# Mixing lora_B by the gate: one plain F32 product against two F32R products of high and low parts

## The reference

```
y = conv1d(x, weight 9 taps, 4 groups) + cond @ c_weight.T + bias
base = y @ kernel (2048x2048) + ffn_bias
A_eff = einsum('bn,nri->bri', gate, lora_A)     # gate 8x16, one-hot
B_eff = einsum('bn,nor->bor', gate, lora_B)     # lora_B 16 x 2048 x 32
delta = B_eff (A_eff y) + lora_B_shared (lora_A_shared y)
out = x + base + delta
```

## Time and profile before

| | us |
|---|---|
| median of 3 runs | 1721.45 (1720.89 to 1723.88) |
| the profiled execution | 1724.4 |
| its span, first to last instruction | 1722.6 |
| TensorE busy | 1705.0 |
| VectorE busy | 1056.6 |
| ScalarE busy | 670.0 |
| TensorE waits of phase 0's convolutions for L997 / L903 | 2.2 / 0.6 |

### The profile page before, as it was taken

One profiled execution on the slowest core, in us unless ns is written; L12 is line 12 of the kernel. 1 busy time (PEld: TensorE's weight loads), 2 busy tenths in 40 slices (PEclk: granted clock), 3 DMA queues, 4 the chain that ended last, 5 costly groups with the idle time before them and its releaser, 6 DMA issues.

```text
span 1722.6 us, 21836 instructions
## 1 busy us (share of the span) xinstructions
PE 1705.0 (99%) x8498; PEld 1442.8 (84%) x8498; DVE 1056.6 (61%) x1428; ACT 670.0 (39%) x846; POOL 37.0 (2%) x70
## 2 busy tenths in 40 slices
PE   8899999999999999999999999999999999999998
PEld 6688888887888898999998888888888888888887
DVE  7677877674444679888886444454555545464443
ACT  6756666644222466566552112132323211121110
POOL 0001111010000000000000000000000000000000
PEclk9899999999999999999999999999999999999999
DMA  7869766675656658776666565577766898887764
GB/s 208 254 213 336 279 229 243 220 268 175 240 211 200 225 200 298 284 258 240 232 236 256 206 248 196 190 221 249 235 223 212 299 335 301 308 316 248 254 235 158
DMA packets 180142, 419.45 MB, mean 244 GB/s; under 512 B 50692, under 2 KB 90212, under 8 KB 175400
## 3 DMA queue, kind: packets, MB, share of 16 engines
q1 hardware_dynamic: 169960, 381.22, 65.1%
q0 software_dynamic: 9216, 33.56, 5.3%
q10 hardware_dynamic: 864, 3.29, 0.5%
HBM read 271.97 MB, written 146.03 MB: 243 GB/s over the span
## 4 chain that ended last, share of the span: by engine, by line
PE 95%; DMA 2%; DVE 1%; ACT 1%; SPq 0%; issue 0%; DVEq 0%; ACTq 0%
PE acc L1487 69%; PE cps L1359 15%; PE cps L1410 3%; PE acc L1394 3%; PE acc L1324 1%; PE acc L1442 1%; DMA g<-in_L_ffn_lora_A 1%; PE cps L1427 1%; DMA b_raw<-mixed_B 1%; ACT x_q L713 0%; PE cps L1420 0%; DMA mixed_B<-b_raw 0%; DMA b_raw<-shared_B 0%; PE acc L1464 0%; DVE w_lo L964 0%
## 5 line engine op out<-in xcount | busy, mean ns | idle before, releaser
L1487 PE MATMUL acc<-w_hi,y_t 128*128 128x512 f32 x3584 | 993.7, 391 | 0.0
L1487 PEld LDWEIGHTS acc<-w_hi,y_t 128*128 128x128 f32 x3584 | 666.5, 188 | 135.9 <-issue 2.7
L1487 PE MATMUL acc<-w_lo,y_t 128*128 128x512 f32 x1792 | 553.7, 390 | 0.0
L1487 PEld LDWEIGHTS acc<-w_lo,y_t 128*128 128x128 f32 x1792 | 337.0, 188 | 71.6
L713 ACT COPY x_q<-x_raw 32x512 f32<-32x512 f32 x248 | 268.5, 1083 | 19.3 <-DVE x_lo L978 13.1
L1359 PE MATMUL cps<-cw,x_hi 128*128 128x256 f32 (+2 forms) x1200 | 263.8, 310 | 0.7 <-DVE x_lo L1155 0.7
L752 ACT CAST y_t<-g 128x1024 fp32r<-128x1024 f32 x95 | 100.1, 1054 | 329.2 <-PE acc L1487 297.9
L1096 DVE TENSOR_TENSOR g<-acc,g 128x1024 f32<-128x1024 f32 x96 | 117.3, 1222 | 178.6 <-PE acc L1394 112.8
L1359 PEld LDWEIGHTS cps<-cw,x_hi 128*128 128x128 f32 x1200 | 194.3, 189 | 14.9 <-issue 12.0
L1359 PE MATMUL cps<-cw,x_lo 128*128 128x384 f32 (+2 forms) x768 | 193.0, 287 | 0.0
L1056 DVE TENSOR_TENSOR y_t<-g,y_t 128x1024 fp32r<-128x1024 f32 x95 | 116.0, 1221 | 102.6 <-ACT y_t L752 102.4
(11 more groups left out here) (122 smaller groups left out, 970.8 us busy)
## 6 DMA issues: line engine op xcount, KB each, us to landing
g<-A SPq DMA_DIRECT2D x80, 512.0 KB, 4.8
g<-U SPq DMA_DIRECT2D x80, 512.0 KB, 6.4
A<-g SPq DMA_DIRECT2D x64, 512.0 KB, 4.0
g<-in_x SPq DMA_DIRECT2D x64, 512.0 KB, 6.3
out<-g SPq DMA_DIRECT2D x64, 512.0 KB, 3.5
x_raw<-in_x SPq DMA_DIRECT2D x31, 1024.0 KB, 5.1
U<-g SPq DMA_DIRECT2D x48, 512.0 KB, 3.7
g<-in_L_ffn_kernel POOLq DMA_DIRECT2D x32, 512.0 KB, 7.7
```

The source lines that it names most:

```text
L1487: ins = T.matmul(acc[:, b, m, :], y_buf[b][:, c, part, :], wt[:, k % SLOTS, m * 512:(m + 1) * 512], start=(c == 0 and part == 0 and wt is ...
```

## The change

G is gone. Its place is taken by gate_hl, the gate's high part in columns 0 to 63 and its low part in columns 64 to 127 of axd_hl[:, 0] (which is used for something else only from phase 4 on). ScalarE's copy_turn rounds the turned block to F32R in b_hi's left half; the new turn_lo subtracts that from PSUM on VectorE, which gives the low part in the right half. mix_B makes two F32R products into all 128 rows of PSUM with the same weights: rows 0 to 63 hold the gate's high part times both, rows 64 to 127 its low part times both. The new copy_mixed_B of ScalarE takes rows 64 to 127 to b_stage, and VectorE's adds rows 0 to 63.

```
-        G = sb("G", [P, NB, R8])
+        gate_hl = axd_hl[:, 0, :].rearrange("p (h b r) -> p h b r", h=2, b=NB)
-        b_turn = b_raw[:, 0:512]
+        b_turn = [b_hi[:, i * 512:(i + 1) * 512] for i in range(2)]
 scalar:
             def copy_turn(q):
                 act.wait_ge(bt_done, q + 1)
-                A.copy(b_turn, cps[:, 0, :]).then_inc(bt_ready, 1)
+                A.copy(b_turn[0], cps[:, 0, :]).then_inc(bt_hi, 1)
+
+            def copy_mixed_B(q):
+                act.wait_ge(bmix_done, q + 1)
+                A.copy(b_stage, cps[NB * R8:P, 1, :]).then_inc(bmix_upper, 1)
...
             copy_turn(0)
+            copy_mixed_B(0)
...
                     split_t(f + 1, EARLY_SPLIT[p])
+                if u < NP:
+                    copy_mixed_B(u)
 vector:
             def copy_mixed_B(q):
-                dve.wait_ge(bmix_done, q + 1)
-                V.tensor_copy(b_stage, cps[0:NB * R8, 1, :]).then_inc(bmix_copied, 1)
+                dve.wait_ge(bmix_upper, q + 1)
+                V.tensor_tensor(b_stage, cps[0:NB * R8, 1, :], b_stage, ALU.add).then_inc(bmix_copied, 1)
+
+            def turn_lo(q):
+                dve.wait_ge(bt_hi, q + 1)
+                V.tensor_tensor(b_turn[1], cps[:, 0, :], b_turn[0].bitcast(F32), ALU.subtract).then_inc(bt_ready, 1)
...
+            V.tensor_copy(gate_hl[:, 0], gate_pair[0][:, :, 0, :]).then_inc(g_hi_ready, 1)
+            dve.wait_ge(g_hi_ready, 1)
+            V.tensor_tensor(gate_hl[:, 1], gate_pair[0][:, :, 0, :], gate_hl[:, 0].bitcast(F32), ALU.subtract
+                            ).then_inc(g_hi_ready, 1)
...
             copy_turned_A(7)
+            turn_lo(0)
             copy_mixed_B(0)
...
+                if u < NP:
+                    turn_lo(u)
                 for j, half in FORM_AT.get(u, ()):
                     form(j, half)
 tensor:
             def mix_B(q):
-                pe.wait_ge(bt_ready, q + 1)
                 if q == 0:
+                    pe.wait_ge(g_hi_ready, 2)
                     pe.wait_ge(aturn_copied, 8)
-                T.matmul(cps[0:NB * R8, 1, :], G[:].rearrange("p b r -> p (b r)"), b_turn, start=True, stop=True
-                         ).then_inc(bmix_done, 1)
+                pe.wait_ge(bt_hi, q + 1)
+                T.matmul(cps[:, 1, :], axd_hl[:, 0, :], b_turn[0], start=True, stop=False)
+                pe.wait_ge(bt_ready, q + 1)
+                T.matmul(cps[:, 1, :], axd_hl[:, 0, :], b_turn[1], start=False, stop=True).then_inc(bmix_done, 1)
```

More of the change, by code:

```diff
@@ L218, in build @@
         bt_done = sem("bt_done")
+        bt_hi = sem("bt_hi")
         bt_ready = sem("bt_ready")
+        g_hi_ready = sem("g_hi_ready")
+        bmix_upper = sem("bmix_upper")
         bmix_done = sem("bmix_done")
@@ L1206, in _ @@
             dve.wait_ge(gpair_zero, 2)
-            for i, dst in enumerate((G[:], gate_pair[0][:, :, 0, :], gate_pair[1][:, :, 1, :])):
+            for dst in (gate_pair[0][:, :, 0, :], gate_pair[1][:, :, 1, :]):
                 V.tensor_tensor(dst, gate_col[:].unsqueeze(2).to_broadcast([P, NB, R8]),
@@ L1226, in _ @@
             V.tensor_copy(axd_hl[R2:P, 1, :], ax_tmp[R2:P, 0:P])
+            dve.wait_ge(g_ready, 1)
+            V.tensor_copy(gate_hl[:, 0], gate_pair[0][:, :, 0, :]).then_inc(g_hi_ready, 1)
+            dve.wait_ge(g_hi_ready, 1)
+            V.tensor_tensor(gate_hl[:, 1], gate_pair[0][:, :, 0, :], gate_hl[:, 0].bitcast(F32), ALU.subtract
+                            ).then_inc(g_hi_ready, 1)
             dve.wait_ge(ones_zero, 4)
@@ L1423, in mix_B @@
             def mix_B(q):
+                if q == 0:
+                    pe.wait_ge(g_hi_ready, 2)
+                    pe.wait_ge(aturn_copied, 8)
+                pe.wait_ge(bt_hi, q + 1)
+                T.matmul(cps[:, 1, :], axd_hl[:, 0, :], b_turn[0], start=True, stop=False)
                 pe.wait_ge(bt_ready, q + 1)
-                if q == 0:
-                    pe.wait_ge(aturn_copied, 8)
-                T.matmul(cps[0:NB * R8, 1, :], G[:].rearrange("p b r -> p (b r)"), b_turn, start=True, stop=True
-                         ).then_inc(bmix_done, 1)
+                T.matmul(cps[:, 1, :], axd_hl[:, 0, :], b_turn[1], start=False, stop=True).then_inc(bmix_done, 1)
             def mix_A(n):
@@ L1433, in mix_A @@
                 if n == 0:
-                    pe.wait_ge(g_ready, 3)
+                    pe.wait_ge(g_ready, 2)
                     pe.wait_ge(ctx_ready, 1)
```

## The result

The changed kernel takes 1728.83 us (median of 7 runs, 1725.09 to 1733.61) against 1721.84 us before (7 runs, 1716.15 to 1723.88): ratio 1.0039, 95% interval 1.0022 to 1.0057: slower by 0.39%. Its profiled execution has a span of 1727.0 us where that of before has 1722.6.

The account below looks back on a forecast made before the run. TensorE, with 95% of the chain, was taken as the bound. Lateness of 8.4 us after step 5, from step 0's hold, half clock and the forms, less 4.7 gained later, gave +3.7: 1725.2 us, range 1719.8 to 1729.9.

Parts of the forecast that it names:

- rival D: Mixing products don't get shorter, so no 0.64 us gain anywhere: +7.5 us, 1728.9; chance 0.06.
- rival C: VectorE, with add and turn_lo, bounds every step; steps 6 to 14 gain nothing: +8.4 us, 1729.9; chance 0.11.
- 0.64 gained per step where nothing waits: Mixing on TensorE: 1.10 us of plain F32 becomes two F32R products, 0.46 us, in each of 16 steps.
- Step 0: 4.27 later: ScalarE's new copy waits for mixing 0 ahead of rearranging x, which starts 4.27 us later; TensorE idles 5.4 us.
- 1.6 for the half clock: Step 0, after TensorE's idling: the halved clock costs 1.5 us, a little more after the longer idling.
- ScalarE's later work is hidden from step 1 on: ScalarE's emptying of the product comes 1.1 us later, but the convolution asks for it only some 4 us on.
- The forms carry the lateness whatever TensorE does: Steps 3 to 5: VectorE's forming of T matrices waits for loads chained to earlier stores, all carrying +6.9 us.
- The branch: Clock holds after step 4's 1.5 us stall, halves after step 5's 2.3: +3.7; otherwise falls at step 4: +2.2, 1723.7.
- Steps 8, 11 and 12: 0.32, 0 and 0.55: Smaller gains in us: VectorE's L997 limits steps 8 and 11; forms and turn_lo hold the add in step 12.
- Step 15 gives nothing: Last mixing: no gain, because TensorE next waits for stored mixed_B, issued from a queue late on its own account.
- B: Copy at step 0 costs nothing, ScalarE reaches the rearrangement in time: faster, 1717.8 us; chance 0.09.
- E: Loads of steps 3 to 5 land up to 2.5 us sooner, partly swallowing step 0's lateness: +1.2, 1722.6; chance 0.14.

Follow-up runs that it names:

- the hold alone: Kernel before, old F32 mixing, with ScalarE at step 0 waiting for mixing 0 and copying 64x512 from PSUM ahead of its rearrangement of x: ratio 1.0046 to before.
- its removal: Changed kernel with only step 0 altered: ScalarE joins behind the emptying of the first product, VectorE adds behind its rearrangement of x: ratio 0.9995 to before.
- Joining on VectorE: Changed kernel with VectorE copying rows 64 to 127 and then adding; ScalarE has no part in the joining: ratio 0.9990 to before.
- turn_lo behind the form: Changed kernel with turn_lo of step 2 behind the first form on VectorE instead of before it: ratio 1.0006 to before.
- without joining: Changed kernel with the gate's low part left out of the result; VectorE copies rows 0 to 63, ScalarE copies nothing: ratio 0.9982 to before.
- the order and the spread forms together: Changed kernel, ScalarE's split of A and joining and VectorE's add reordered, forms spread over more steps: ratio 0.9933 to before.
- changed, forms spread: Changed kernel with nothing but the forms spread, half a form in each step from 1 to 8: ratio 0.9972 to before.
- mixing twice: Changed kernel with each mixing computed twice over, four F32R products of 512 columns instead of two: ratio 1.0069 to before.
- the own order: Changed kernel; ScalarE splits A before the emptying, joins behind it; VectorE adds behind rearranging x except in steps 2 to 5, 12 to 15: ratio 0.9981 to before.

## Why the prediction was right, and where its sizes were off

The direction and the mechanism held, and the measured time is inside the range: +3.7 us forecast, +7.0 measured by the medians (ratio 1.0039, interval 3.8 to 9.8 us). The sum was built on the profiled execution of before. Against it the profiled execution of the changed kernel took 4.4 us more (1728.83 and 1724.4), while the distance from mixing 0 to mixing 15 grew by 5.3. Mixing 0 itself came 1.33 us sooner in it. The 7 runs of the changed kernel span 8.5 us, those of before 7.7, so the medians and the two executions can't be held to each other more closely than that. After step 5 the lateness was 9.6 (8.4 forecast), and the steps behind gained 4.2 (4.7 forecast).

The measured 1728.83 lies nearer to rival D (1728.9) and rival C (1729.9) than to the forecast of 1725.2. That is coincidence: neither mechanism is in the trace, as the rivals behind the list show. Step by step:

- *0.64 gained per step where nothing waits.* Right, a little small: 0.72 in steps 6, 10 and 13: 0.63 between product and convolution and 0.11 at the convolution's first pair, behind which the next matmul now begins sooner; why is not shown. The page "Perfetto Trace Analysis" of the Trainium skill, section "Engine Utilization", halves the matmul peak for FP32_LOW_HIGH. The prediction had set aside the reading by which a whole plain F32 product costs only two F32R ones, and the runs agree with it: 1.01 us from start to start before, 0.46 now.
- *Step 0: 4.27 later.* 4.22. The hold of ScalarE's queue was computed from five rows and is shown by the hold alone and by its removal. ScalarE kept the order of its queue: L716 began at 76.97, behind the copy that waited.
- *1.6 for the half clock.* Mis-sized: 2.85 in the changed kernel, 1.4 with the hold alone. The row used was the stall of step 4 of before, where the clock was back at full 3 us after the stalled matmul of 182.96 (first line below). In the changed kernel it stayed at half for over 6 us, until nearly 93, and in the hold alone it was back before 90 (second and third line). Since a convolution follows in both, the work behind the stall does not explain the difference. Of the 1.6 us by which 5.3 exceeds 3.7, this term is 1.2, the largest part.

```profile
186.00:187.00 1.00, 1.00 (x5) 0.77 (x5) 0.97 (x3) 0.36 (x1) 0.00 (x0) 0.99 0.07 23
...
88.00:90.00 2.00, 2.00 (x10) 2.00 (x10) 1.02 (x3) 0.00 (x0) 0.00 (x0) 0.58 0.99 303
90.00:92.00 2.00, 2.00 (x16) 2.00 (x16) 1.21 (x3) 0.00 (x0) 0.00 (x0) 1.00 0.72 275
```

- *ScalarE's later work is hidden from step 1 on.* Wrong in steps 1, 7 and 9: the split of A comes later, VectorE waits 0.66 for it, and L1008 is late for TensorE. They gained 0.30 each where 0.64 was forecast: 1.0 in sum. Joining on VectorE, with steps 1, 7 and 9 at 21.97, shows it.
- *The forms carry the lateness whatever TensorE does.* Right from step 3 to 5 in the changed kernel: the first form was 8.4 later against mixing 0 (6.9 forecast, the 1.5 being the two items above), step 5's L1008 9.7. The branch was wrong: the clock fell after the stalls of steps 3 and 4 (2.90 and 2.67 us), and step 5 waited only 0.58. Since the forms set the end of that stretch, it changed little. Turn_lo's own part, 1.64 forecast, is the 1.68 that turn_lo behind the form took back. "Whatever TensorE does" was too strong: the hold alone and turn_lo behind the form both show loads that came in time.
- *Steps 8, 11 and 12: 0.32, 0 and 0.55.* 0.22, -0.09 and 0.58.
- *Step 15 gives nothing.* It lost 1.0. What TensorE's operand waited for last was not mixed_B but shared_B, reloaded right behind it into the same buffer: it was issued 3.6 us later, close to the 4.0 of mixing 15, and landed 6.74 us after that instead of 5.35. In order of time, before and changed:

```profile
426.76 5.35 DMA b_raw<-shared_B
...
430.37 6.74 DMA b_raw<-shared_B
```

The distance from mixing 15 to that product was 18.3 to 19.0 us in the three kernels with the old mixing and 18.7 to 20.1 in the eleven with the new one. I count the 1.0 as mostly the DMA's scatter; that the change has no part in it is not shown.

Together 5.3 us until mixing 15, with the 1.0 behind it 6.3 up to the first product with lora_B. The rivals: B (the hold costs nothing) is excluded by the hold alone. C (VectorE in every step) is excluded by steps of 21.97 without joining, where turn_lo is in, and by steps 1, 7 and 9 of 21.97 with the whole joining on VectorE. D (the products don't get shorter) is excluded by the 0.46 us. E (loads that land sooner against the forms) is not seen in the changed kernel, with 24.84 and 26.60 from form to form, but it is what the hold alone showed, with 22.70 where before had 24.64: a part of a late start can come back there, in some executions.

## What to carry to other kernels

An instruction added to a queue costs what stands behind it, not what it takes: 0.58 us of copy cost 7, since eight copies and an emptying that TensorE needed stood behind its wait in one step of sixteen. Look through an added wait step by step, the first step above all, where the order differs; and look at which engine serves the waiting one next (the split of A), because moving the wait may only move the stall. Where a stretch is paced by loads that follow each other's stores, gains elsewhere in it can vanish until that chain is spread; here the order and the spread forms together turned +0.39% into -0.67%.

## What the runs showed that I had not expected

The cost of TensorE idling besides the idling itself does not follow the length of the idling. Stalls in step 0 of 4.72 us (hold alone), 5.00 (changed), 5.15 (turn_lo behind the form), 6.30 (changed, forms spread) and 6.32 (mixing twice) made the convolution 1.4, 2.85, 2.7, 2.4 and 2.15 us longer than the 4.91 of before. With the spread forms the clock fell while TensorE still idled, so that part of the half clock cost nothing; without joining it was still at 1.00 just before the 3.92 us stall ended, and 0.54 only afterwards. Changed with forms spread (stall over at 85.26), then without joining (over at 159.12):

```profile
84.00:85.00 1.00, 0.00 (x0) 0.00 (x0) 0.00 (x0) 0.98 (x2) 0.00 (x0) 0.50 1.15 263
...
157.00:159.00 2.00, 0.00 (x0) 0.00 (x0) 1.90 (x5) 0.00 (x0) 1.33 (x3) 1.00 0.93 307
159.00:161.00 2.00, 1.88 (x6) 1.59 (x7) 1.93 (x5) 0.98 (x2) 0.78 (x2) 0.54 1.04 410
```

Nor does the clock fall after every such stall. It fell after 2.20 us in step 4 of before, but a stall of 3.06 us in step 5 of the own order left it at 1.00:

```profile
207.52 0.50 PE L1352 MATMUL acc<-cw,x_hi 128*128 128x256 f32 x2 [3.06 <-DVE g L1012]
```

```profile
208.00:210.00 2.00, 2.00 (x11) 1.60 (x10) 1.93 (x5) 1.86 (x2) 0.00 (x0) 1.00 0.99 414
```

The wait of 2.1 us ahead of mixing 0 (2.10 to 2.15) stands in all fourteen executions; in seven of them, before and changed among these, the clock fell to half behind it, in the other seven it stayed at full. So the prediction's "After such idling the clock is at half" held in step 0 of the changed kernel, but it is no rule of these runs, and a term of this kind deserves a range from nothing to nearly 3 us.

And the 64x512 copy from PSUM took 0.58 us on ScalarE, that of 128x512 0.59: here half the rows saved nothing.
